# A convolution and feed-forward kernel: square roots with a constant epsilon, and a seventh normalised column on ScalarE in three chunks of eight

## What is computed

```
_ln_c(v): (v - mean) / sqrt(var + 1e-6) over the 96 channels of a pixel
_ln_t(v): (v - mean) / sqrt(var + 1e-5) over the 96 channels of a pixel
x = x + conv3x3(_ln_c(x)) + _ln_c(x)         # depthwise, kernel per channel
t = x as tokens (one per pixel)
t = t + ffn(_ln_t(t))                        # 96 -> 384 -> relu -> 96, fp8 (e5m2) factors
```

## Time and profile before

| what | value |
|---|---|
| time, median of 3 runs | 3360.18 us (3359.96 to 3365.55) |
| time of the profiled execution | 3365.72 us |
| its span, first to last instruction | 3364.0 us |
| busy: DVE, ACT, PE, POOL | 95%, 93%, 90%, 57% of the span |
| mean granted TensorE clock | 0.974 |
| HBM traffic | 211 GB/s over the span |

### The profile page before, as it was taken

How to read it: one execution, slowest core, us unless ns; L and a number is a source line. 1 busy time by engine, 2 the same in 40 slices (tenths; PEclk the granted TensorE clock), 3 DMA queues, 4 the chain that set the end, 5 groups by cost and what they waited for, 6 DMA issues and landing times.

```text
span 3364.0 us, 87592 instructions
## 1 busy us (share of the span) xinstructions
PE 3014.8 (90%) x24902; PEld 2505.1 (74%) x24902; DVE 3211.1 (95%) x11767; ACT 3142.8 (93%) x7072; POOL 1921.2 (57%) x915
## 2 busy tenths in 40 slices
PE   5689999899998999989999899989999999999877
PEld 5577777777777777777777777777777777778744
DVE  8559999999999999999999999999999999999998
ACT  7779999999999999999999999999999999987776
POOL 0005666556665666656666566656666666666676
PEclk9999999999999999999999999999999999999966
DMA  6777777777776777777777777767777777776533
GB/s 219 213 201 216 225 225 225 216 223 222 224 224 206 224 227 228 223 208 226 223 222 225 208 225 225 229 203 226 224 224 222 225 229 223 225 201 183 157 120 99
DMA packets 277528, 714.48 MB, mean 212 GB/s; under 512 B 35001, under 2 KB 35106, under 8 KB 277026
## 3 DMA queue, kind: packets, MB, share of 16 engines
q1 hardware_dynamic: 271394, 694.12, 70.5%
q10 hardware_dynamic: 5632, 14.45, 1.3%
HBM read 539.84 MB, written 168.59 MB: 211 GB/s over the span
## 4 chain that ended last, share of the span: by engine, by line
DVE 66%; issue 14%; PE 9%; ACT 8%; DMA 2%; DVEq 1%; SPq 0%; ACTq 0%; POOL 0%; POOLq 0%
DVE stats L654 22%; DVE xq L691 19%; DVE hid L644 10%; PE conv_ps L434 6%; DVE hid L649 5%; DVE images L703 5%; ACT images L526 3%; ACT hid L505 3%; DVE xt_ps L678 2%; PE hid_ps L397 1%; DVE rstd L682 1%; DVE neg_mean L686 1%; DVEq L183 1%; PE y_ps L412 1%; DVE y L671 1%
## 5 line engine op out<-in xcount | busy, mean ns | idle before, releaser
L434 PE MATMUL conv_ps<-images,band_ring 112*112 112x222 f32 (+1 forms) x8928 | 1884.4, 356 | 29.8 <-DMA band_ring<-bands 29.5
L434 PEld LDWEIGHTS conv_ps<-images,band_ring 112*112 112x112 f32 x8928 | 1553.2, 178 | 180.5 <-issue 31.9
L279 POOL TENSOR_TENSOR xf<-xf,y 112x768 f32<-112x768 f32 x448 | 952.0, 2125 | 1174.3 <-DVE y L671 1174.3
L505 ACT ACTIVATE hid<-hid_ps 128x896 f16<-128x896 f32 x1344 | 1191.9, 928 | 91.6 <-PE hid_ps L397 88.3
L274 POOL TENSOR_TENSOR xf<-xf,images 112x768 f32<-112x768 f32 x448 | 981.4, 2191 | 264.4 <-ACT images L537 246.7
L526 ACT ACTIVATE images<-xn,neg_mean,rstd 112x96 f32<-112x96 f32 x2590 | 1044.5, 556 | 21.3 <-DVE neg_mean L686 16.8
L412 PEld LDWEIGHTS y_ps<-w2t,hid 128*128 128x128 f16 x10752 | 576.4, 100 | 410.7 <-ACT hid L505 221.6
L412 PE MATMUL y_ps<-w2t,hid 128*128 128x96 f16 x10752 | 672.9, 210 | 210.8 <-ACT hid L505 186.9
L691 DVE SCALAR_TENSOR_TENSOR xq<-xf,stats,xt_ps 112x96 fp8e5<-112x96 f32 x3584 | 843.7, 317 | 0.0
L397 PE MATMUL hid_ps<-xt,w1t 96*128 96x448 fp8e5 x2688 | 684.1, 364 | 24.0 <-ACT xt L497 24.0
L644 DVE TENSOR_SCALAR hid<-hid,b1q 128x896 f16<-128x896 f16 x1344 | 594.6, 473 | 16.4 <-ACT hid L505 15.3
(11 more groups left out here) (55 smaller groups left out, 824.6 us busy)
## 6 DMA issues: line engine op xcount, KB each, us to landing
band_ring<-bands SPq DMA_DIRECT2D x744, 294.0 KB, 5.1
xf<-in_x SPq DMA_DIRECT2D x462, 336.0 KB, 5.0
out<-xf SPq DMA_DIRECT2D x448, 336.0 KB, 3.8
xn<-in_x SPq DMA_DIRECT2D x434, 336.0 KB, 3.4
bands<-images ACTq DMA_DIRECT2D x16, 882.0 KB, 8.0
xf<-bands SPq DMA_DIRECT2D x24, 294.0 KB, 4.4
xf<-in_L_ffn_W SPq DMA_DIRECT2D x2, 144.0 KB, 3.1
xf<-in_L_conv_kernel SPq DMA_DIRECT2D x3, 3.4 KB
```

The costliest lines, as they stand in the source:

```text
L279: pool.tensor_tensor(res, res, y[:, e % 2], ALU.add).then_inc(summed, CW)
L434: mm = pe.matmul(dst[:, :, lo:hi], band_place(t < CONV_AT + UNIT, n)[:, PAIR * dx + i, :], images[:, m % 2, :, ch, lo + dx - 1:hi + dx - 1 ...
L505: nc.scalar.activation(hid[:, e % 2, TOK * j:TOK * (j + 1)].rearrange("p (u n) -> p u n", u=2), hid_ps[:, k, :, 0:HALF * H], ACT.Identity) ...
```

## The change

`act_cols` gives ACT a seventh column in three chunks of eight (those with n mod 8 = 2, 5 and 7), for all chunks after the first 28; DVE is left with one column there. The column is added at the end of ACT's second group, ahead of the cast of the first third. The bound of the second group becomes the chunk's width, and the increment of the semaphore moves with it. Both square roots take epsilon as a constant of the instruction, and the tile `eps`, its two memsets and their semaphore increment go (so the counts that are waited for on `consts` fall by one).

```diff
+MORE, EVERY = 3, 8
...
-        eps = sb("eps", [H, 2], F32)
...
         def act_cols(n):
-            return FIRST_ACT_COLS if n < UNIT else ACT_COLS
+            return FIRST_ACT_COLS if n < UNIT else ACT_COLS + MORE * (n % EVERY + 1) // EVERY - MORE * (n % EVERY) // EVERY
...
-                for i, v in enumerate((EPS_T, EPS_C)):
-                    op = pool.memset(eps[:, i:i + 1], v)
-                op.then_inc(consts, 1)
...
-                def normalise(r, n, lo, hi):
+                def normalise(r, n, lo, hi, first=False, last=False):
                     b, i, cols = chunk_at(n)
-                    if lo == 0:
+                    if first:
...
-                    hi = min(hi, act_cols(n))
-                    for w in range(lo, hi):
+                    for w in range(lo, min(hi, act_cols(n))):
...
-                    if hi == act_cols(n):
+                    if last:
                         op.then_inc(normed[0], 1)
...
                     nc.scalar.activation(std[:, e % 2, 0, :], stats[:, e % 2, 0, :, 2], ACT.Sqrt,
-                                         bias=eps[:, 0:1], scale=1.0 / C).then_inc(std_t_done, 1)
+                                         bias=EPS_T, scale=1.0 / C).then_inc(std_t_done, 1)
...
                     nc.scalar.activation(std[:, n % 2, 1, :], stats[:, n % 2, 1, :, 2], ACT.Sqrt,
-                                         bias=eps[:, 1:2], scale=1.0 / C).then_inc(std_c_done, 1)
+                                         bias=EPS_C, scale=1.0 / C).then_inc(std_c_done, 1)
...
-                        normalise(r, c + 1 + LOOP, 0, ACT_COLS // 2)
+                        normalise(r, c + 1 + LOOP, 0, 3, first=True)
                     save_conv(r, c, t, 0, 1)
                     if norm_in(t + 1):
-                        normalise(r, c + 1 + LOOP, ACT_COLS // 2, ACT_COLS)
+                        normalise(r, c + 1 + LOOP, 3, CW, last=True)
```

More of the change, by code:

```diff
@@ L46, in metaformer @@
     assert B % IMGS == 0 and 2 * GROUPS % BAND_RING == 0
-    assert 2 * UNIT % NORM_RING == 0 and 2 * UNIT % FFN_RING == 0
+    assert 2 * UNIT % NORM_RING == 0 and 2 * UNIT % FFN_RING == 0 and 2 * UNIT % EVERY == 0
     assert FIRST_NORM_RING % NORM_RING == 0 and GROUPS % FIRST_BAND_RING == 0
@@ L251, in _ @@
                 pool.memset(taps_16, 0.0).then_inc(consts, 1)
-                pool.wait_ge(consts, 5)
+                pool.wait_ge(consts, 4)
                 for k, rows in enumerate(part_rows):
                     if k:
-                        pool.wait_ge(consts, 5 + 2 * k)
+                        pool.wait_ge(consts, 4 + 2 * k)
                     pool.affine_select(out=shift[rows, :], in_=ones[rows, :], pattern=[[1, 2 * H]],
@@ L261, in _ @@
                                        channel_multiplier=-1).then_inc(consts, 1)
-                pool.wait_ge(consts, 11)
+                pool.wait_ge(consts, 10)
                 pool.affine_select(out=ident[:, :], in_=ident[:, :], pattern=[[1, P]], compare_op=ALU.is_equal,
@@ L350, in _ @@
             def _(pe):
-                pe.wait_ge(consts, 14)
+                pe.wait_ge(consts, 13)
                 pe.wait_ge(prep, 2)
@@ L600, in _ @@
                 dve.wait_ge(taps_sem, 16 * PARTS)
-                dve.wait_ge(consts, 14)
+                dve.wait_ge(consts, 13)
                 for rows in part_rows:
```

## The result

The changed kernel takes 3394.9 us (median of 4 runs, 3391.1 to 3401.8), the kernel before 3360.1 beside it (3355.1 to 3365.6): a ratio of 1.0104, with a 95% interval of 1.0089 to 1.0118. **It is slower by 35 us, 30 to 40 with the interval**; 3385, or 25 more, was forecast. The two profiled executions have spans of 3364.0 and 3389.4 us and differ by 25.4, but that of the kernel before (3365.7) is 5 us above the median of its runs, and that of the changed kernel (3391.1) the fastest of four. So this match with the forecast is chance; the medians count.

What follows compares the result with a forecast made beforehand. DVE at 6.94 us a step bounds the kernel, barely above a circle of ACT and PE (6.90). The change makes that circle the bound at 7.00: +0.06 to +0.07 in 391 steps, +25 us, 3385 us; range 3338 to 3404.

Steps and rivals of the forecast that it cites:

- Who bounds the kernel before: Steady part before the change: DVE at 6.94 us a step, just above ACT and PE's closed way, mean 6.90.
- The circle and its place: ACT's columns, first cast, PE's matmuls, cast of y, back to ACT: mean 6.90 us before, 7.00 after.
- The seventh column: On ACT ahead of the first cast: lengthens five of seven kinds of step by its whole 0.36 us.
- The column taken from DVE: DVE's work: one column less, 0.24 us, in three chunks of eight; mean step falls 0.09 to 6.85.
- The roots: ACT behind the first cast: 0.11 us saved each, 0.22 a step; only two 4-channel kinds gain, 0.05 each.
- PE's 3.64: From the first cast to the cast of y: PE's way takes 3.64 us, ACT's own work 3.60.
- The sum: Whole kernel: 7.00 us a step against 6.94, +25 us over 391 steps, 3385 us.
- the +0.065 of the steady step: Growth of the mean step, 6.94 to 7.00 us, put at +0.06 to +0.07 in each of 391 steps.
- PE's wait for the first cast: On PE in 3-channel steps with seven columns: 0.36 us longer than the 0.77 before.
- faster: Rival: ACT's total work counts, not its way over PE; DVE's 6.85 stays the bound, 3325 us; chance 0.20.
- The same: Rival: ACT and PE's closed way costs less than added up; 6.94 or 6.95 a step, 3360 us; chance 0.12.
- Slower by more: Rival: no slack, each step costs the larger bound; 7.07 us a step, +49, 3409 us; chance 0.12.

Runs made afterwards that it cites:

- The run at the crossing: The changed kernel with the seventh column in one chunk of eight in place of three; 3362.4 us, ratio 1.0006 to the kernel before.

## Why the prediction was right

- **Who bounds the kernel before.** DVE at 6.94 by a hair: held up. In the trace of before, 344 of the 377 steps of DVE from 300 to 2950 us lie between 6.91 and 6.95 us; in the changed kernel it is 101 of 373. And the roots alone, with DVE's work untouched, stay within 4 us, though ACT has 74 us less to do.
- **The circle and its place.** The steps reckoned at 7.05, 6.93 and, with the seventh column, 7.41 are in the trace of after, its steps at their shortest have the mean of 7.00 that was reckoned, and 0.19 us of equal work costs 57 us ahead of the first cast and 14 behind it.
- **The seventh column**, 0.36 in the circle: 1.43 for four where 1.07 was for three.
- **The column taken from DVE**, 0.24: DVE's step is 6.70.
- **The roots.** The saving was put at 0.11 each and is 0.09 to 0.10; a root takes 0.10 and not 0.08. Beside PE's 3.64 it brings nothing, as forecast: the pair of casts stands for 1.82 where 1.8 was said. The Trainium skill's page ScalarE: Activation LUTs ("What ACT_TABLE_LOAD costs") has 93 ns for each pointer operand. The traces agree: mean durations of 311 and 214 ns differ by 97, so the page's figure was nearer than my 110. The price was right; that ACT's work on the whole is the bound, which the rival added to it, was not.
- **The sum**, +25 us, came out too small: by the medians it is +35, interval 30 to 40. The term that is too small is the +0.065 of the steady step; it is 0.086 (6.937 to 7.023), which is 8 of the missing 10 us. The circle's 7.00 was right. I took the larger of two means and left out what the two lose to each other: the circle's short steps can't be short when DVE, at 6.94 with its two columns, isn't there yet. In the changed kernel the steps of 3 channels with six columns and no copy in the middle are 6.60 at their shortest and 6.71 on the mean, which is 7 of the 8 us. One of 7.00 us, from 1627.45 on, seen on PE:

```profile
1630.14 0.64 PE L409 MATMUL y_ps<-w2t,hid 128*128 128x96 f16 x11 [0.23 <-DVE hid L645]
...
1634.05 0.37 PE L377 MATMUL xt_ps<-ident,xq 112*128 112x112 bf16 x4 [0.43 <-DVE xq L687]
```

That the profiled spans give +25.4, the very sum of the forecast, is luck: the ten steps where a round begins took 5 us less in the changed kernel's trace, and one of the two executions was a slow one of its kernel, the other the fastest. The run at the crossing loses 12 us in the same way.
- **Said of the profile and wrong:** DVE was to idle 2% in the steady part; it shows 0.8% (4.2 of 500 us). Its work of 6.85 in steps of 7.02 leaves 2.4% of waiting, so most of it doesn't show as idle time: where instructions overlap, a short wait only moves the next start. And PE's wait for the first cast was to be 0.36 longer; it is 0.67 longer than the 0.77 of the earlier trace rows, because I had not seen the 0.34 us for which PE waited for DVE earlier in that step.

The rivals: *faster* falls with the two places of the same work. *The same* falls with the interval. *Slower by more* (49 us, no slack at all between DVE and the circle) is beyond the interval too; the truth lies between it and the forecast, nearer the forecast: there is some slack, but less than the forecast took. The Trainium skill's page Perfetto Trace Analysis, section "Identifying the Most-Contended Engine", says to optimise the engine with the highest occupancy first. Here that was DVE at 95%; it was relieved by 0.09 us a step, and the kernel lost 1%.

## What to carry to other kernels

When several engines are over 90% busy, follow one step from start to start and write down each closed way over two engines; moving work to the engine with less of it can help only if its new place lies off the longest circle. Look for the pair of points between which another engine's way is longer: what you save between them is lost, and what you add ahead of them is paid nearly in full (0.17 of 0.19 us in the 3-channel steps here). Where two bounds lie close, expect more than the larger of their means: 0.02 to 0.03 us a step here. And before an instruction is moved that frees a buffer, read what is queued behind the transfer that waits for it: 0.22 us won in a step of 7.41 were given back in steps that waited for loads of other data. No run here won time by moving a column.

## What I had not expected

The order of issues on SP is worth far more than the change under study. One load put behind two that wait for PE cost 470 us (3864.8 against 3394.9), and the load's landing time went from 3.5 to 5.1 us when it was issued between others. I had counted SP as free because it does no computing.
